# A depthwise convolution's second channel block for one batch: TensorE with folded weights instead of VectorE's taps

## The reference, cut to what matters

```python
xz = jnp.einsum('bld,ed->ble', x, in_w)              # x is RMS-normed, 128 wide; xb and z 256 wide each
xb, z = jnp.split(xz, 2, axis=-1)
xc = lax.conv_general_dilated(xb.transpose(0, 2, 1), cw[:, None, :], window_strides=(1,),
        padding=[(D_CONV - 1, 0)], ..., feature_group_count=D_INNER)   # 4 taps, one filter per channel
xb = jax.nn.silu((xc + cb[None, :, None]).transpose(0, 2, 1))
dbc = jnp.einsum('ble,re->blr', xb, xp_w)            # low-rank delta, B and C
delta = softplus(dbc[..., :8] @ dtw + dtb)
```

## Time and profile before

| | |
|---|---|
| runs, us | 1098.5, 1099.05, 1104.31; median 1099.05 |
| profiled execution, device time | 1103.25 us |
| its span | 1101.9 us |
| what lies around the span | 1.35 us |
| busy share of the span | PE 93%, DVE 88%, ACT 74%, PEld 58%, POOL 47% |
| mean granted TensorE clock | 0.955 of full |

### The profile page before, as it was taken

One profiled execution on the slowest core, in us unless ns is written; L12 is line 12 of the kernel. 1 busy time (PEld: TensorE's weight loads), 2 busy tenths in 40 slices (PEclk: granted clock), 3 DMA queues, 4 the chain that ended last, 5 costly groups with the idle time before them and its releaser, 6 DMA issues. The chain is left out here.

```text
span 1101.9 us, 21377 instructions
## 1 busy us (share of the span) xinstructions
PE 1022.4 (93%) x7821; PEld 641.6 (58%) x7821; DVE 971.3 (88%) x1308; ACT 819.3 (74%) x1596; POOL 521.1 (47%) x488
## 2 busy tenths in 40 slices
PE   6899999999999978989999998899999996779997
PEld 3122222222222334468998885458888884479997
DVE  5999999999996688979999997889999999888885
ACT  4289999999999646978888853988888871348761
POOL 4501401010101342037898993028999995147773
PEclk9679999999999998799999999899999998779999
DMA  4230101000000542108999990107999994912223
GB/s 116 70 94 17 31 16 30 18 24 24 17 2 2 136 96 41 59 6 198 241 249 226 224 233 1 58 5 174 221 245 240 217 254 145 266 53 74 71 73 127
DMA packets 60328, 121.04 MB, mean 110 GB/s; under 512 B 15486, under 2 KB 28798, under 8 KB 59968
## 3 DMA queue, kind: packets, MB, share of 16 engines
q0 software_dynamic: 15440, 52.66, 24.0%
q1 hardware_dynamic: 43170, 64.98, 19.0%
q10 hardware_dynamic: 1614, 2.04, 0.6%
HBM read 58.02 MB, written 13.19 MB: 65 GB/s over the span
## 5 line engine op out<-in xcount | busy, mean ns | idle before, releaser
L2315 PEld LDWEIGHTS m_pair<-filter_w,delta_x_t 128*128 128x128 f32 x2560 | 294.0, 192 | 43.2 <-issue 43.2
L2315 PE MATMUL m_pair<-filter_w,delta_x_t 128*128 128x112 f32 (+3 forms) x2560 | 298.6, 276 | 9.6 <-DVE h_t L2342 3.3
L571 DVE TENSOR_REDUCE neg_max<-max_ps 128x1 f32<-128x1024 f32 x256 | 292.9, 1210 | 10.1 <-PE max_ps L560 9.8
L688 ACT ACTIVATE exp_scores<-score_k 128x512 f32<-128x512 f32 x512 | 274.0, 600 | 15.7 <-PE score_k L680 8.3
L2291 ACT ACTIVATE decay<-delta,a_log 128x1024 f32<-128x1024 f32 x128 | 145.8, 1142 | 49.9 <-DVE normed L2342 29.5
L560 PE MATMUL max_ps<-k_rows,q_rows 48*128 48x512 bf16 x512 | 166.3, 403 | 6.5 <-DVE neg_max L571 5.6
L2283 ACT ACTIVATE filter_w<-filter,b_t 128x112 f32<-128x112 f32 (+1 forms) x576 | 167.4, 375 | 0.0
L708 PE MATMUL score_k<-exp_scores,v_cols 128*32 128x256 f32 x2048 | 164.1, 394 | 0.0
L680 PE MATMUL score_k<-q_rows,k_rows 51*128 51x512 bf16 x512 | 162.8, 389 | 0.0
L580 POOL CAST neg_max_parts<-neg_max 128x16 bf16<-128x16 f32 x16 | 3.1, 196 | 233.2 <-DVE neg_max L571 233.2
L560 PEld LDWEIGHTS max_ps<-k_rows,q_rows 48*128 48x128 bf16 x512 | 29.8, 95 | 119.6 <-DVE neg_max L571 91.4
(11 more groups left out here) (346 smaller groups left out, 1731.7 us busy)
## 6 DMA issues: line engine op xcount, KB each, us to landing
c_row<-c_rows SPq DMA_DIRECT2D x64, 512.0 KB, 6.4
x_inner<-normed POOLq DMA_DIRECT2D x16, 512.0 KB, 6.8
delta_x<-mod_memory POOLq DMA_DIRECT2D x15, 512.0 KB, 9.2
delta_x<-x_inner POOLq DMA_DIRECT2D x15, 512.0 KB, 8.6
x_inner<-h_t POOLq DMA_DIRECT2D x14, 512.0 KB, 5.7
mod_memory<-h_t POOLq DMA_DIRECT2D x14, 512.0 KB, 9.5
mod_memory<-normed POOLq DMA_DIRECT2D x12, 512.0 KB, 9.1
gate_up_all<-in_gate_up_w SPq DMA_DIRECT2D x8, 512.0 KB, 7.4
```

Of the source, the lines that this page charges most:

```text
L571: ve.tensor_reduce(nm[leg % 2][:, 4 * j + qt:4 * j + qt + 1], mps[:, bank:bank + 2, :].rearrange("p a q -> p (a q)"), AX_X, ALU.max, negat ...
L688: ac.activation(pt[a % 4][:, HEADS[r % 4], :], eps[:, bank, :], ACT.Exp, scale=SC).then_inc(*exped.up())
L2315: mm = pe.matmul(vps[blk][:, lo:hi], self.duT[b][:, c, blk * P:(blk + 1) * P], wf[g % 3][:, lo:hi], start=True, stop=True)
```

## The change

For layer 0's chunks 0 and 1 the second block goes the way of the first: four accumulating matmuls with the folded weights of that block, then bias and Silu from PSUM. `pe_last_block`, the copy (L1645) and the taps on VectorE are no longer issued for these two chunks. Chunks 2 and 3, and all of layer 1, keep both ways. `pe_first_block` now waits for its chunk's turn itself.

```diff
-        def pe_first_block(c, bank):
+        def pe_first_block(c, bank, blk=0):
             b, off = chunk[c]
+            pe.wait_ge(*ht[c])
             pe.wait_ge(*self.taps_set[l])
             wait_from(pe, *bank.open)
             for j in range(KW):
-                mm = pe.matmul(bank.ps[:], cw[l][:, j, 0:P], hp[:, b, off + j:off + j + CH],
+                mm = pe.matmul(bank.ps[:], cw[l][:, j, blk * P:(blk + 1) * P], hp[:, b, off + j:off + j + CH],
                                start=(j == 0), stop=(j == KW - 1))
             mm.then_inc(bank.full[0], 1)
 
-        def ac_conv_first(c, bank):
+        def ac_conv_first(c, bank, blk=0):
             b, off = chunk[c]
             ac.wait_ge(*bank.full)
-            ac.activation(xb[:, 0, b, off:off + CH], bank.ps[:], ACT.Silu, bias=cb[:, l, 0:1]).then_inc(bank.left[0], 1)
-            conv[0, c] = bank.left
+            ac.activation(xb[:, blk, b, off:off + CH], bank.ps[:], ACT.Silu,
+                          bias=cb[:, l, blk:blk + 1]).then_inc(bank.left[0], 1)
+            conv[blk, c] = bank.left
...
+        def pe_conv(c):
+            for blk in range(NBLK):
+                bank["f", c, blk] = ring.take()
+                pe_first_block(c, bank["f", c, blk], blk)
+
+        def ac_conv(c):
+            for blk in range(NBLK):
+                ac_conv_first(c, bank["f", c, blk], blk)
...
         if l == 0:
             turn(0)
             turn(1)
-            pe_l(0)
-            ac_last_block(0, bank["l", 0])
-            pe_l(1)
-            ac_last_block(1, bank["l", 1])
-            ve_taps(0, bank["l", 0])
-            pe_f(0)
-            ve_taps(1, bank["l", 1])
-            ac_conv_first(0, bank["f", 0])
-            pe_f(1)
-            ac_conv_last(0)
+            pe_conv(0)
+            ac_conv(0)
+            pe_conv(1)
             pe_x(0)
-            ac_conv_last(1)
-            ac_conv_first(1, bank["f", 1])
+            ac_conv(1)
             self.ve_mamba_center(1)
             self.ve_mamba_shift(2)
             ac_low(0, bank["x", 0])
```

## The result

| | before | changed |
|---|---|---|
| first measurement, median us | 1100.83 (6 runs) | 1106.89 (6 runs) |
| ratio, 95% interval | | 1.0051 (1.0032 to 1.0070) |
| second measurement, on another chip, median us | 1116.77 (26 runs) | 1121.27 (12 runs) |
| ratio, 95% interval | | 1.0038 (1.0019 to 1.0057) |
| profiled execution: device time, span | 1103.25, 1101.9 | 1105.94, 1104.6 |

The forecast was +4.75 us, or 0.43%. The two ratios mean +5.6 and +4.2 us, each with some 2 us either side. Both chips are slower with the change; whether by over or under 0.5% lies inside the intervals.

A forecast was written before the change was run, and what follows sets the result against it. VectorE bounds the stage, TensorE only 0.29 us behind. Twelve more passes (5.15 us), less that room and a 0.10 us wait, delay it 4.75 us; 1099.05 + 4.75 = 1103.8 us, range 1099.5 to 1108.5 us.

The forecast's parts named there:

- The bound and its room: Where ScalarE's queue joins both engines, the stage waits for VectorE; TensorE's result is ready only 0.29 us before its use.
- Passes: On TensorE ahead of the low-rank product: 32 passes instead of 20, 12 more at 0.429 us, 5.15 us.
- The order: On ScalarE, batch 1's squares queue among low-rank copies, which wait behind all 32 TensorE passes; stage late by 4.75 us.
- VectorE's relief: Two chunks of taps removed from VectorE, 5.6 us; its shifts end 5 us earlier, but the gain becomes idle time.
- Further on: Everything behind batch 1's last square and chunk 1's low-rank copy, through the scan, moves by the same 4.75 us.
- rival D: Overlooked slack between 437 and 480 us absorbs the 4.75 us; time 1099 to 1100 us, chance 0.05.
- The clock: TensorE's granted clock keeps both low stretches of the profiled execution; taken as 0, between -2.1 and +3.4 us.
- A: Kinder clock: one or both low stretches vanish or shrink; +2.7 us, 1101.7 us, chance 0.16.
- B: Harsher clock: a low stretch lies over fp32 passes that nothing covers; +3.4 us more, 1107.2 us, chance 0.18.
- the same two pauses: TensorE idles 1.07 us before L1743 and 1.81 us before L411, each followed by a clock fall; both forecast to return.
- Rival C: The two passes of each fp32 matmul overlap when run on end on TensorE; faster, 1095.2 us, chance 0.04.
- The footing: The +4.75 us was added to the three-run median, 1099.05 us, not the profiled execution, which was 4.2 us slower.

The follow-up runs named there:

- e5: The changed kernel with three of the four taps of the second block of chunks 0 and 1 left out; ratio 0.9994 to the kernel before.
- e1: The kernel before with 12 more TensorE passes ahead of chunk 0's low-rank product, VectorE's taps and ScalarE's copies kept; ratio 1.0042 to the kernel before.
- e3: Half of the change: chunk 0's second block stays on VectorE's taps, chunk 1's goes to TensorE; ratio 1.0028 to the kernel before.
- e2: The changed kernel with VectorE's eight tap instructions of chunks 0 and 1 put back, their result unread; ratio 1.0059 to the kernel before.
- e4: The changed kernel with batch 1's two squares ahead of chunk 1's Silu and both low-rank copies in ScalarE's queue; ratio 1.0042 to the kernel before.
- e10: The changed kernel with batch 1's squares, transposes, projections and taps brought forward, its Silu ahead of the Ln on ScalarE; ratio 1.0037 to the kernel before.

## Why the prediction was right

- **The bound and its room.** The 0.29 us between TensorE's result and ScalarE's use of it was read off right; e5 measured 0.29 us.
- **Passes.** 12 more at 0.429 us are 5.15 us, and the low-rank product's start moved by 5.15 us, to 433.22 us. The forecast of 433.11 us had taken 0.10 us off for a wait that would go. The gain did not show: 32 passes on end took 0.4325 us each. So the delay of the norms is 4.85 us and not 4.75. The price holds in e1 and e3 as well.
- **The order.** Low(0), low(1) and square(3) were forecast at 435.03, 436.75 and 437.37 us and came at 435.14, 436.85 and 437.47; the norms at 440.95 against about 440.9. Square(2) did stand idle behind low(0).
- **VectorE's relief is given away.** Shown: 9.40 us of idle time, and e2, with the work put back, has its norms at the same 21.58 us.
- **Further on.** "The whole stage starts from this point" held to the first scan instruction (+5.03 us), so rival D is out. e4 shows that the stage starts by two chains, of which the prediction followed the one and only named the other.
- **The clock.** In the profiled execution of the changed kernel neither A nor B showed. The first low stretch came again inside the second of the same two pauses, as before, now from 440.9 to 447.7 us, and the denser 32 passes did not keep it away:

```profile
440.90:447.70 6.80, 6.32 (x14) 3.34 (x15) 5.85 (x14) 5.37 (x8) 0.02 (x1) 0.51 0.01 2
```

  The 8 transposes took 1.94 us again and the 16 carry passes 5.30 us against 5.37. That was partly luck. The second low stretch came back in two parts, 461.3 to 464.7 and 468.1 to 471.5 us, and the second part happened to lie over the carry passes. In e2, e3, e4, e5 and e10 no low stretch did: the passes that A had priced at 3.63 us instead of 5.37 took 3.61 us, and the way from their start to the scan was some 1.4 us shorter (22.15 us in e2 against 23.58 in the kernel before). It does not follow the length of the dense run: e5 has 20 passes on end and had the gain, the changed kernel has 32 and had it in neither of its two profiles. By the rule of the Trainium skill that the prediction names ("Perfetto Trace Analysis", "Matmul Optimizations") the longer dense run should have helped the clock. Neither profile of the changed kernel bears that out.
- **Rival C** fell with the first row: 32 passes on end cost 0.4325 us each.
- **The footing.** 1103.8 us was built on a median of 1099.05 us from three runs; with six it was 1100.83. Of the 3.1 us between forecast and measured median, 1.8 lie there, and the rest is inside the interval of the ratio (3.5 to 7.7 us). The time was in the range. The times alone would not settle a difference of 1 or 2 us; the rows do.

## What to carry to other kernels

Before moving work from one busy engine to another, measure how far apart the two arrive at the place where they meet; here it was 0.29 us, so 5.6 us taken from the one were worth 0.3 at most, and the passes given to the other were paid in full but for those 0.3. Then look at the in-order queue at that meeting place: an early result behind a late one is a late result, and moving one chain forward only helps if the other chains through that queue move too. For a change of a few microseconds in a thousand, compare the starts of one instruction after a common first one, not two spans, and look at the granted clock over the rows between.

## What the runs showed that was not expected

- The granted clock's low stretches fall at other places from one execution to the next. In e5 one lay over nearly all of 412 to 419.3 us, where the kernel before had full clock, and the stage began 2.7 us later; VectorE's rows of the two stood within 0.6 us of each other up to 417 us. That the clock did it is the likely reading; no run isolates it.

```profile
412.00:419.30 7.30, 6.67 (x26) 5.17 (x27) 6.41 (x19) 3.10 (x5) 1.84 (x2) 0.56 1.20 171
```

- Chips differ on the same kernel before, by 16 us: 1100.83 and 1101.16 us in two measurements, 1116.77 and 1116.93 us on two other chips. Where those 16 us lie was not looked for.
